# B*dt*u of three states per sequence by turned, scaled copies in a state-space recurrence, with its preparation laid out anew

## What is computed

```python
xz = x @ W_in.T;  xi, z = split(xz)
u = silu(causal_conv4(xi) + conv_b)
x_dbl = u @ W_x.T                        # dt (rank 4), B (16), C (16)
dt = softplus(x_dbl[..., :4] @ W_dt.T + b_dt)
A = -exp(A_log)
h = exp(dt[..., None] * A) * h + (dt * u)[..., None] * B[:, None, :]   # per step
y = einsum('bdn,bn->bd', h, C) + u * D_skip
out = y * silu(z) @ W_out.T
```

## Time and profile before

| | us |
|---|---|
| median of 3 runs (756.58 to 759.8) | 759.32 |
| profiled execution | 756.54 |
| its span, first to last instruction | 754.4 |
| POOL busy in the span | 473.5 |
| DVE busy | 570.3 |
| PE busy (matmuls) | 599.6 |
| ACT busy | 440.6 |

### The profile page before, as it was taken

The page is one execution under the profiler, slowest core; times in us unless marked ns, Lnnn a source line. Parts: engine busy times, 40 slices in busy tenths (PEclk is TensorE's granted clock), DMA queues, the critical chain, the costliest instruction groups (busy, mean ns, idle before and its releaser), DMA issues.

```text
span 754.4 us, 10800 instructions
## 1 busy us (share of the span) xinstructions
PE 599.6 (79%) x3563; PEld 253.5 (34%) x3591; DVE 570.3 (76%) x589; ACT 440.6 (58%) x662; POOL 473.5 (63%) x254
## 2 busy tenths in 40 slices
PE   4866786787887777967868787978986969999994
PEld 2311121221221112312212222446663335777751
DVE  4498998998998999999989998445562435666643
ACT  3977577578578567676685752444544224555521
POOL 6379999999999999999999999500003200000002
PEclk9998798899998998998989999999999889999997
DMA  3499576576576676775775662000001110000001
GB/s 98 103 290 316 196 252 233 215 244 237 199 257 200 235 257 217 234 237 199 251 238 202 255 227 87 1 1 2 2 11 46 45 44 1 2 1 2 1 1 60
DMA packets 34009, 107.48 MB, mean 142 GB/s; under 512 B 7061, under 2 KB 7582, under 8 KB 33950
## 3 DMA queue, kind: packets, MB, share of 16 engines
q1 hardware_dynamic: 31382, 102.89, 40.7%
q10 hardware_dynamic: 1928, 2.65, 1.1%
q0 software_dynamic: 640, 1.18, 0.5%
HBM read 98.84 MB, written 4.19 MB: 137 GB/s over the span
## 4 chain that ended last, share of the span: by engine, by line
PE 40%; issue 17%; DVE 16%; POOL 15%; ACT 6%; DMA 3%; SPq 1%; DVEq 0%; POOLq 0%; ACTq 0%
POOL hc L1763 8%; POOL dbu L1774 7%; DVE hh_all L1463 6%; PE py L229 6%; PE pb L198 6%; PE px L252 5%; PE py L714 5%; DVE pb L1458 4%; PE pb L925 2%; PE px L741 2%; DMA cc<-scr 2%; PE pb L702 1%; PE px L242 1%; PE py L949 1%; DVE yg L1472 1%
## 5 line engine op out<-in xcount | busy, mean ns | idle before, releaser
L1763 POOL TENSOR_TENSOR hc<-hh_all,cc 128x1024 f32<-128x1024 f32 x128 | 298.0, 2347 | 2.3 <-DVE hh_all L1463 1.3
L714 PE MATMUL py<-hc,w_cst 64*64 64x512 f32 x1024 | 153.3, 658 | 26.9 <-POOL hc L1763 17.1
L1463 DVE TENSOR_TENSOR_SCAN hh_all<-da,pb 128x1024 f32<-128x1024 f32 x72 | 164.6, 2286 | 2.5
L1777 POOL TENSOR_TENSOR yg<-w_xs 128x512 f32<-128x512 f32 x10 | 12.7, 1266 | 239.3 <-DVE w_xs L1599 153.0
L1463 DVE TENSOR_TENSOR_SCAN hh_all<-pb,dbu 128x1024 f32<-128x1024 f32 x56 | 127.7, 2280 | 17.5 <-POOL dbu L1774 14.1
L1774 POOL TENSOR_TENSOR dbu<-bb,dtu_all 128x1024 f32<-128x1024 f32 x56 | 131.5, 2349 | 0.0
L702 PE MATMUL pb<-bc,w_sel 128*128 128x512 bf16 x118 | 41.8, 421 | 71.6 <-DVE hh_all L1463 67.6
L1169 ACT ACTIVATE pb<-dt_all,w_aneg 128x1024 f32<-128x1024 f32 x56 | 62.6, 1118 | 58.3 <-DVE hh_all L1463 56.7
L1458 DVE TENSOR_TENSOR pb<-pb,dtu_all 128x1024 f32<-128x1024 f32 x72 | 87.5, 1215 | 1.8 <-DVE dtu_all L1444 0.2
L285 DVE TENSOR_REDUCE gate_all<-pb 128x1 f32<-128x1024 f32 (+7 forms) x64 | 60.4, 985 | 29.6 <-PE pb L208 14.8
L1169 ACT ACTIVATE da<-dt_all,w_aneg 128x1024 f32<-128x1024 f32 x72 | 80.5, 1137 | 0.5
(11 more groups left out here) (292 smaller groups left out, 951.2 us busy)
## 6 DMA issues: line engine op xcount, KB each, us to landing
cc<-scr SPq DMA_DIRECT2D x128, 512.0 KB, 4.4
bb<-scr SPq DMA_DIRECT2D x56, 512.0 KB, 4.7
out<-yg ACTq DMA_DIRECT2D x8, 256.0 KB, 2.5
w_xs<-hc SPq DMA_DIRECT2D x6, 256.0 KB, 4.5
w_xst<-in_x SPq DMA_DIRECT2D x2, 512.0 KB, 5.3
scr<-bcf SPq DMA_DIRECT2D x8, 128.0 KB, 3.7
w_xs<-dt_all SPq DMA_DIRECT2D x4, 256.0 KB, 5.6
w_xs<-dtu_all SPq DMA_DIRECT2D x4, 256.0 KB, 5.9
```

What stands on the lines that cost most here:

```text
L714: last = nc.tensor.matmul(py[part(t), half(r)], ident[part(r), part(r)], hc[u % NHC][part(r), half(t)], start=(n == 0), stop=(n == NS - 1) ...
L1463: nc.vector.tensor_tensor_scan(hh[u % NHH][:, :], decay[:, :], drive[:, :], 0.0, ALU.mult, ALU.add).then_inc(scan_done, 1)
L1763: nc.gpsimd.tensor_tensor(hc[u % NHC][:, :], hh[u % NHH][:, :], cc[u % NCC][:, :], ALU.mult).then_inc(hc_done, 1)
```

## The change

- Three of 16 states per sequence become *crossed*. ACT holds dtu turned (time on the partitions: dtu_t, 8 blocks of 128 x 128) and B turned (b_t). For a crossed unit it makes 8 copies of 128 x 128, each scaled by a per-partition column of b_t, into cross (act_cross); PE turns the 8 blocks back into pb (pe_cross); DVE scans with no product of its own.
- Pooled states become 6 of 16, own ones 7 of 16. Which ones depends on the sequence: sequence 0 and the odd ones below the last have the preparation one state later (shifted) and another list.
- The own rows are spread by float32 matmuls of 64 rows, one for each half of the time axis in its own half of the array (row tiles), with a one-hot column of the constants as the stationary operand. w_sel, the bfloat16 parts, the two subtractions and their four kinds of ACT copies go; one float32 copy of B and C (bcs) stays and feeds the DRAM scratch as well.
- Added for each sequence: turning dtu (8 transposes on PE, 2 copies on ACT) and B (4 transposes, 1 copy).
- The preparation moves in each queue, and the output products of sequence pairs (pe_out_early, pe_out_late) both stand at n = 15 instead of 13 and 14, with ACT's copies of them at n = 0 of the next sequence. The start of the kernel has less on DVE (no copies of B) and on POOL (no w_sel, no w_less).

```diff
-        POOLED = (1, 4, 6, 8, 10, 12, 14)
+        POOLED, CROSSED = ((1, 3, 6, 8, 11, 13), (1, 3, 5, 8, 10, 13)), ((5, 10, 15), (6, 11, 15))
+        def shifted(q):
+            return 1 if q == 0 or (q % 2 and q < LAST) else 0
+        def cross_step(u):
+            return u - (3 if u % NS == NS - 1 and shifted(u // NS) else 2)
+        def pe_b_t(pe, s):
...
+            for j in range(4):
+                last = nc.tensor.transpose(b_turned_at(s)[:, block_at(j)], bcs[s % 2][:, block_at(j)], ident)
+        def pe_dtu_t(pe, s):
+            for h in range(2):
+                pe.wait_ge(px_free[h], freed(s) + 2 if s else 1)
+                for j in range(4):
+                    last = nc.tensor.transpose(px[h][:, block_at(j)], dtu[s % 2][:, block_at(4 * h + j)], ident)
+                last.then_inc(dtu_turned, 1)
+        def pe_cross(pe, u):
+            atleast(pe, scan_done, u - 1)
+            pe.wait_ge(cross_done, cross_count(u) + 1)
+            for j in range(8):
+                last = nc.tensor.transpose(pb[u % 2][:, block_at(j)], cross[:, block_at(j)], ident)
+            last.then_inc(cross_full, 1)
         def pe_b(pe, u):
...
+            if crossed(u):
+                pe_cross(pe, u)
+                return
...
-                last = nc.tensor.matmul(pb[u % 2][:, half(h)], w["sel"][:, n, :], bc3[q % 2][:, half(h)], start=True, stop=True)
+                last = nc.tensor.matmul(pb[u % 2][:, half(h)], cst[part(h), SELV + n:SELV + n + 1].broadcast_to((C, 128)),
+                                        bcs[q % 2][part(h), :], start=True, stop=True)
+        def act_cross(act, u):
+            q, n = divmod(u, NS)
+            act.wait_ge(b_t_done, q + 1)
+            act.wait_ge(dtu_t_done, 2 * q + 2)
+            atleast(act, cross_full, cross_count(u))
+            for j in range(8):
+                last = nc.scalar.activation(cross[:, block_at(j)], dtu_t[:, block_at(j)], ACT.Copy, scale=b_t[:, q % 2, 2 * (j % 4) + j // 4, n:n + 1])
+            last.then_inc(cross_done, 1)
...
+                        if n == 13 + o and h == 0:
+                            pe_dtu_t(pe, q + 1)
-                        if n == 13 and h == 0:
-                            pe_out_early(pe, q // 2 - 1)
-                        if n == 14 and h == 0:
-                            pe_out_late(pe, q // 2 - 1)
+                    if q % 2 == 0 and q > 0 and n == 15 and h == 0:
+                        pe_out_early(pe, q // 2 - 1)
+                        pe_out_late(pe, q // 2 - 1)
...
+                if crossed(u):
+                    dve.wait_ge(cross_full, cross_count(u) + 1)
+                else:
+                    k = own_count(u)
+                    dve.wait_ge(b_full, k + 1)
+                    nc.vector.tensor_tensor(pb[u % 2][:, :], pb[u % 2][:, :], dtu[q % 2][:, :], ALU.mult).then_inc(dbu_done, 1)
```

More of the change, by code:

```diff
@@ L395, in build_all @@
         yg = [sb(f"yg_{i}", [DI, L]) for i in range(2)]
-        bc3 = [sb(f"bc3_{i}", [128, L], BF16) for i in range(2)]
-        bcf = sb("bcf", [32, L])
+        bcs = [sb(f"bcs_{i}", [128, HALF]) for i in range(2)]
         da = [sb(f"da_{i}", [DI, L]) for i in range(NDA)]
@@ L406, in build_all @@
         ex, rl = sb("ex", [DI, L]), sb("rl", [DI, L])
+        dtu_t, cross, b_t = sb("dtu_t", [128, L]), sb("cross", [128, L]), sb("b_t", [128, 2, L // 128, NS])
         pb = [ps(f"pb_{i}", [DI, L]) for i in range(2)]
@@ L987, in _ @@
                 pe_var(pe, 1, h)
[L988 to L989 removed]
+            pe_b_t(pe, 0)
             for h in range(2):
                 pe_dt_add(pe, 0, h)
[L992 to L994 removed]
+            pe.wait_ge(sel_done, 1)
+            pe.wait_ge(sd_done, 4)
             pe_b(pe, 0)
@@ L1163, in act_exp @@
             else:
-                k = own_count(u)
+                k = da_count(u)
                 if k >= NDA:
-                    behind = next(v for v in range(u - NDA, -1, -1) if not pooled(v) and own_count(v) == k - NDA)
+                    behind = next(v for v in range(u - NDA, -1, -1) if not pooled(v) and da_count(v) == k - NDA)
                     act.wait_ge(scan_done, behind + 1)
@@ L1169, in act_exp, with act_dtu_t, act_b_t @@
             nc.scalar.activation(to[:, :], dt[q % 2][:, :], ACT.Exp, scale=w["aneg"][:, n:n + 1]).then_inc(da_done, 1)
+        def act_dtu_t(act, s):
+            atleast(act, cross_done, cross_count(NS * s))
+            for h in range(2):
+                act.wait_ge(dtu_turned, 2 * s + h + 1)
+                nc.scalar.activation(dtu_t[:, half(h)], px[h][:, :], ACT.Copy).then_inc(dtu_t_done, 1)
+        def act_b_t(act, s):
+            act.wait_ge(b_turned, s + 1)
+            nc.scalar.activation(b_t[:, s % 2, :, :], b_turned_at(s).rearrange("p (j r) -> p j r", r=C)[:, :, 0:NS], ACT.Copy).then_inc(b_t_done, 1)
+        def act_cross(act, u):
[6 more added lines that the diff above has]
+            last.then_inc(cross_done, 1)
         def act_out(act, b, h):
@@ L1922, in sp_scratch @@
                     sp.wait_ge(bb_in[i], 16 * ((NP * (s - 1) + 1 - i) // 2))
-            sp.dma_start(scr[s % 2, :, :], bcf[:, :]).then_inc(scr_in, 16)
+            for h in range(2):
+                sp.dma_start(scr[s % 2, :, half(h)], bcs[s % 2][C * h:C * h + 32, :]).then_inc(scr_in, 16)
         def sp_c(sp, u):
@@ L2039, in constants @@
     t[:, CAUS:CAUS + 128] = np.where(r[None, :] <= r[:, None], 0.0, -1e30)
-    for part in (0, 64, 96):
+    for part in (0, 64):
         t[part:part + 32, SELV:SELV + 32] = np.eye(32)
```

201 lines of the change are left out of this document (95 added, 106 removed).

## The result

The changed kernel takes 771.1 us in the median, the kernel before 759.0 us on the same chip: the ratio is 1.0163, 95% interval 1.0135 to 1.019, so it is 1.6% slower. The forecast was 739, range 733.5 to 750. The profiled execution took 771.0 us (span 769.2), that of before 756.5 (span 754.4).

| stretch | before, us | after, us | difference |
|---|---|---|---|
| start to GpSimd's first product with C | 46.2 | 46.0 | -0.2 |
| the recurrence, to the end of the last such product | 424.3 | 431.5 | +7.2 |
| from there to the end of VectorE's last instruction | 275.3 | 277.5 | +2.2 |
| from there to the end of the span | 8.6 | 14.3 | +5.7 |

A forecast was written before the change was run, and what follows sets the result against it. POOL was taken to bound the recurrence, 23 operations of 2.31 us per sequence. 756.5 - 18.5 - 1.2 + 0.5 + 1.0 = 738.3 us for the profiled execution; 739 for the median, range 733.5 to 750.

The forecast's parts named there:

- GpSimd's part, -18.5: Recurrence: one drive fewer in each of 8 sequences, 22 x 2.31 = 50.9 us per sequence, 18.5 us saved in all.
- It counts in full as long as POOL never waits: Recurrence: condition on the 18.5 us saving; a late scan stalls POOL only when over about 2.3 us late.
- The other crossed states have an ACT with less before it. So I put them at nothing: Crossed units other than state 5 of an even sequence: their waits for ACT's copies cost 0 us.
- State 5 of an even sequence: Crossed unit's chain: pooled exp(3) delays u, gate matmul, sum and y; 1.2 us late within 1.4 of slack, cost 0.
- ScalarE: right: ACT in the recurrence: 0.30 us per scaled copy, 2.4 per crossed unit, 42.3 us of work in 50.9 per sequence.
- TensorE: nearly right: PE in the recurrence: own row 0.96 us, eight transposes 1.02, work from 42.6 to 48 us per sequence; it fits in 50.9.
- rival 4: Float32 rows on PE: array halves run one behind the other, 6.3 us more per sequence; chance included in the first rival's 0.16.
- Output products, +1.0, ends 0 and 6: Sequences 2, 4 and 6, products together at n = 15: 0.3 us lost per place, 1 us in all.
- Start, -1.2: Kernel start: without DVE's casts of B the first scan comes about 1.2 us sooner; ends 0 and -2.5.
- Behind the recurrence nothing changes: 0: Everything after the recurrence: no change in time, 0 us.
- The first: Rival: POOL stalls through PE and ACT in the recurrence, 1.3 us per sequence, 10 us more, 749; chance 0.16.
- The second: Rival: each crossed unit holds DVE in the recurrence, 2.4 us per unit, slower than before at 775; chance 0.07.

## Why the prediction was wrong

By its own steps, against the profiled executions (forecast -18.2, measured +14.5). The sum ends at 738.3 for the profiled execution; with the 2.8 us by which the median of before lay above its own, it gives 741.1 for the median, not 739. Measured from there the miss is 30 us.

- **GpSimd's part, -18.5: right as an amount of work.** 48 drives and 128 products; eight drives fewer at the measured pitch of 2.31 are 18.5 us. The pitch in the changed kernel, without the waits behind the first product, is (431.5 - 26.5) / 175 = 2.31 us.
- **"It counts in full as long as POOL never waits": here it failed.** GpSimd's waits went from 2.5 to 27.0 us, +24.5; without the one before the first product, which isn't in the recurrence, from 1.1 to 26.5, +25.4. That takes the -18.5 and 6.9 more, of the 7.2 measured. The forecast judged the cushion by VectorE's scans alone (2.3 us, two products queued ahead). The product has a second condition, a free hc, which TensorE's sum gives back; and the sum's place in TensorE's queue, behind the transposes of a turned state, is what the change made worse. 13.0 us of 25.6 are waits for a free hc, the longest at the three places shown above; with the order of transposes and sums turned round 7.4 us of recurrence came back.
- **"The other crossed states have an ACT with less before it. So I put them at nothing": wrong.** Only state 5 of an even sequence was worked through. At state 11 of a shifted one ScalarE has softplus pieces, an exponential and the copies in a row, TensorE waits 4.84 us and GpSimd 1.6. The forecast's own line, that the cover gone costs 24 us for a microsecond of each, was the measure to go by: with each state's copies 1.3 us shorter, 13.3 us came back.
- **State 5 of an even sequence: the chain was right, its price wrong.** It had y late by "1.2 us of lateness out of 1.4 of slack up to drive 6: it costs nothing". In sequence 4 VectorE's y waits 2.59 us for the sum and GpSimd 1.35 and 0.5 behind it. One pooled state moved by one is worth 8.2 us, more than the 4.3 of waits seen at states 2 and 3. The table above shows waits at states 10, 13 and 14 fall with it; that they are the same lateness, paid for later in the sequence, fits this and was not shown by itself.
- **ScalarE: right.** 192 copies in 58.4 us are 0.30 each (forecast 0.30), eight in 2.43; load 42.3 and 41.7 of 53.2 (forecast 42.3). The Trainium skill ("ScalarE: Activation LUTs", What ACT_TABLE_LOAD costs) has 386 ns for a lone one with its column, and says that neighbours overlap by about 93 ns, which makes a pitch of 293 ns, an estimate. The trace agrees with both: a mean duration of 387 ns, and a pitch of (2.43 - 0.39) / 7 = 0.29 us. The 44.4 us of work that the forecast worked out by the 386 ns left the overlap out. What was wrong was to read 42.3 us of work in 50.9 as room.
- **TensorE: nearly right.** Eight transposes 1.09 us (1.02), 1.94 at half clock; an own row 1.13, 1.06 from its start to the next (0.96). The two halves of the array do overlap, so rival 4 is out. Load 44.9 and 45.9 with clocks of 0.97 and 0.94, below the 48 of the forecast. Its 36.8 and 42.3 at full clock don't follow from its row: 12% of 53.2 us at half clock is 6.4 us and gives back 3.2, which makes 39.4 and 44.9.
- **Output products, +1.0, ends 0 and 6:** three waits of 1.2 to 1.5, 4.1 us, inside the bounds. Moving them gained 1.0.
- **Start, -1.2: measured -0.2.** VectorE's casts went, but GpSimd's first product is at 45.97 (before: 46.23). In other kernels with the same code up to there it begins at 44.8 to 46.1, so one execution doesn't settle this term. **First sequence, +0.5, ends 0 and 3:** the wait for a C row is 3.0 instead of 1.0; taken away in another kernel, it turned up nine states later.
- **"Behind the recurrence nothing changes: 0": wrong by 7.9 us,** outside all bounds. 5.7 of it is the branch. 2.2 lie before: TensorE's last output products come 5.5 instead of 4.25 us after GpSimd's last product (4.26 also with seven pooled states and none turned, 5.9 with ten own ones, so it goes with what the last units are); a spell of lower clock moved, from the stretch 20 to 50 us behind GpSimd's last product to that 80 to 90 us behind it, in the first attention layer; the rest, 0.8, comes behind that and isn't assigned. Of before, and then of the changed kernel:

```profile
490.00:520.00 30.00, 24.63 (x165) 14.64 (x161) 15.39 (x32) 14.28 (x34) 0.00 (x0) 0.94 0.00 1
550.10:560.10 10.00, 7.27 (x69) 5.27 (x67) 7.29 (x15) 5.06 (x12) 0.00 (x0) 1.00 0.10 20
```

```profile
497.00:527.00 30.00, 24.54 (x180) 14.99 (x180) 16.78 (x35) 14.77 (x35) 0.36 (x1) 1.00 0.00 1
557.00:567.00 10.00, 7.37 (x59) 5.65 (x56) 5.84 (x11) 4.54 (x10) 0.00 (x0) 0.83 0.10 20
```

  One spell fewer is worth -1.5 us, one more +1.6, so they cancel here; which of them a kernel gets, no experiment settled.

**The rivals.** The first named the right mechanism (buffers of hc, late y, late crossings) and priced it at 1.3 us a sequence; it was 24.5 / 8 = 3.1. It had 0.16, so the mechanism was seen and its size was not. The second, the turned states holding VectorE, wasn't it: VectorE waited for their transposes 4.2 us in all, three times. Its longest waits, 13.9 us for own rows and 12.9 for the sums of y, were for TensorE, as the forecast's sign of being wrong had it. No case held something behind the recurrence. Without the 7.9 us there the program would have taken 763, still 24 above the forecast.

## What to carry over

When a step hands a queue a new wait, list what stands behind it in that queue and who needs it, for every place where it occurs, not for the one that was worked out: the wait itself cost little, and the sums behind it cost 7 us. An engine that has always been busy stays the metronome only as long as each of its conditions has a cushion; a shorter period takes from all of them at once. A change that adds instructions ahead of a loop can lengthen a branch in it, so look at the end of the span and at the queue's own records before looking for a cause in the work.

## What the runs showed of the hardware

- A branch of TensorE's queue that closes a loop took 0.2 us or 7.1 to 7.6 us in kernels with the same work, by the number of TensorE instructions ahead of it (+180 and +692: long; +0, +208, +272 and +768: short). Two other branches took 3.3 to 4.3 us, with the long one or without it.
- A semaphore increment in TensorE's queue cost 0.08 to 0.09 us where 76 stand in a row ahead of its first instruction, and nothing that can be told where they are handed out one or two to a unit: 180 of them moved the recurrence of the kernel before from 424.3 to 424.5 us.
- ScalarE's 128 x 128 copies with a scale per partition took 0.39 us each and followed each other at 0.29 us.
- The granted clock in the first attention layer differed between kernels that have the same code there: 0.69 against 1.00 over ten microseconds in which TensorE was busy throughout; the stretch that holds them was 3.3 us longer. It is as large as many an edit, and only the view by stretches shows it.
